# Second attention: four key steps added up before their sum, by GpSimd and DVE

## The chip, the cores and the metric

The kernel runs on one core of a Trainium2 chip. The metric is the device time of one execution in microseconds (us). TensorE (PE in the profile, its weight loads PEld), VectorE (DVE), ScalarE (ACT), GpSimd (POOL) and SyncE (SP, which only issues transfers here) run side by side and meet at semaphores.

## What is computed

Two layers work on x of shape (2, 2048, 256). The first is a linear attention gated by a transformer block with causal softmax attention and a mixture of experts. The second, which the change touches, is this (float32, 16 heads, real and imaginary halves of 16 kept as one head width of 32):

```python
xn = _layernorm(x, axis=-1)
scores = (einsum('bhnd,bhmd->bhnm', q_r, k_r) + einsum('bhnd,bhmd->bhnm', q_i, k_i)) / sqrt(hd)
scores = where(causal, scores, -inf)
probs = softmax(scores, axis=-1)
out = concatenate([einsum('bhnm,bhmd->bhnd', probs, v_r), einsum('bhnm,bhmd->bhnd', probs, v_i)], -1)
s = out @ Wo
g = silu(x_n @ quantized_kernel + bias + (x_n @ a) @ b)
x = x + s * g
```

## The kernel before

The stages run one after another: preparation and the linear attention, the first softmax attention (`narrow_attention`, to about 1290 us), gate, experts and projection, then `wide_attention` (about 2300 to 3410 us), and `finish`, which divides by the softmax sums, projects and adds.

`wide_attention` treats 2 batches of 16 heads as 8 groups of four heads (HG = 4). A unit (g, u) is a group and a block of 512 queries (QB); there are 32 units. A step (unit, kc) is one tile of 128 keys of a unit; unit u has 4u + 4 of them, 320 in all, the last four on the diagonal, where only 512, 384, 256 and 128 query columns are left. The work of a unit, by the names of the schedule:

- S: a score tile with queries on the partitions (line 839, with its mask at 842), 1280 of them; DVE takes the maximum over its keys from PSUM (line 802) and frees one of three PSUM slots. M closes a unit's maxima, T turns them into a row (876, copied at 824), and SyncE's transfers put the row beneath the queries, so that the next products come out with the maximum subtracted.
- ST: a score tile with keys on the partitions for one head (851, 855), four per step; ACT takes its exponential (787) into a slot of `probs`.
- PV: values times probabilities of the step, four heads in four strips of 32 columns of the array (902), into `acc_ps`.
- A: GpSimd adds the probabilities of two neighbouring steps into `added` (751). SM: TensorE sums `added` over keys with a matrix of ones (915); on the diagonal the first 128 columns, which the second step doesn't have, are taken from `probs` (919).
- EV: ACT copies a finished `acc_ps` (764) or `sum_ps` (769) out, and SyncE stores it.

The order of all this is written out ahead by `wide_schedule` (line 477 on), a planner that keeps an end time for each engine and at every turn takes the kind of work on TensorE that could start soonest; each engine then runs its own share of that one list in the list's order. `probs` is a ring of four steps (RING = 4) and `added` has two slots:

```python
mm = pe.matmul(sum_ps[32 * h:32 * h + 32, both:QB], C["ones32"][:, :],
               added[:, totals % 2, h, both:QB], start=kc == 0, stop=False)
```

An exponential into a slot waits for the PV of the step that lay there, and for its addition or, for the first step of a diagonal pair, its sum (`released_by_sums`).

Of the kernel before, what the change touches and what calls it, by code (L numbers as in the profile page):

```python
# [4 lines left out]
F32 = mybir.dt.float32  # L5
# [466 lines left out]
def released_by_sums(step):  # L472
    (g, u), kc = step
    return kc >= 4 * u and kc % 2 == 0


def wide_schedule():
# [31 lines left out]
    exp_end, pv_end, row_at, add_end, sum_end = [], [], {}, [], []  # L509
    at = n_item = n_pair = n_quad = n_sum = of_unit = 0  # L510
# [9 lines left out]

    def lead():
# [6 lines left out]
    while at < len(ahead) or n_quad < len(steps) or 2 * n_sum < len(steps):  # L528
        choice = []
        turn = lambda to: SWITCH if mode != to else 0  # L530
        if at < len(ahead):
# [5 lines left out]
            if g < 2 or n_quad > last_of[g - 2]:  # L537
# [3 lines left out]
                choice.append((start + (500 if lead() > 2 else 0), 0, "S", start))  # L541
        if n_pair < len(steps) * HG:
            s, quad = steps[n_pair // HG], n_pair // HG
            old = quad - RING
            held = old >= 0 and (n_sum if released_by_sums(steps[old]) else len(add_end)) <= old // 2
            if n_pair % (2 * HG) == 2 * HG - 1 and n_sum < quad // 2 - 1:
                held = True
            if s[0] in row_at and quad - n_quad < RING and not held:
                start = max(pe, st_free[n_pair % ST_SLOTS] + 60, row_at[s[0]]) + turn(16)
                choice.append((start, 1, "ST", start))  # L550
        if n_quad < len(steps) and HG * (n_quad + 1) <= n_pair:
# [6 lines left out]
            choice.append((start + 150, 2, "PV", start))  # L558
        if n_sum < len(add_end):
            s = steps[2 * n_sum]  # L560
            ready = add_end[n_sum] + 60
# [4 lines left out]
            choice.append((start + 150, 3, "SM", start))  # L566
        _, _, kind, start = min(choice)
# [20 lines left out]
        elif kind == "ST":  # L588
# [6 lines left out]
            old = quad - RING  # L595
            needs = 0.0 if old < 0 else 220 + max(
                pv_end[old], (sum_end if released_by_sums(steps[old]) else add_end)[old // 2])
# [5 lines left out]
            if h == HG - 1 and quad % 2:  # L603
                body.append(("A",) + s)
                free_tile = sum_end[quad // 2 - 2] if quad // 2 >= 2 else 0.0
                pool = max(pool, act + 100, free_tile + 100) + HG * w * 2.2 + 100
                add_end.append(pool)
        elif kind == "PV":
# [5 lines left out]
            n_quad += 1  # L614
            if s[1] == 4 * s[0][1] + 3:
                body.append(("EV", s[0], 0))
                evictions.append((pe, 0))
        else:
            s = steps[2 * n_sum]
            body.append(("SM",) + s)  # L620
            mode = 32
            pe = start + width2(s) * COLUMN * 4 + 50
            sum_end.append(pe)
            n_sum += 1
            if s[1] == 4 * s[0][1] + 2:
# [5 lines left out]
def wide_attention(nc, tag, C, q_hi, q_lo, k_hi, k_lo, v, out, sums):  # L631
# [13 lines left out]
    steps = [(unit, kc) for unit in units for kc in range(4 * unit[1] + 4)]  # L645
# [3 lines left out]
    with Ctx(nc, tag) as c:  # L649
# [3 lines left out]
        probs = c.sb("probs", [P, RING, HG, QB], F32)  # L653
        added = c.sb("added", [P, 2, HG, QB], F32)
# [25 lines left out]
        add_done = c.sem("add_done")  # L680
        sum_done = c.sem("sum_done")
# [57 lines left out]
        def _(pool):  # L739
            pairs = n = 0  # L740
            for ev in body:
                if ev[0] == "ST":
                    pairs += 1
                elif ev[0] == "A":
                    _, (g, u), kc = ev
                    off = max(0, kc - 4 * u) * P
                    quad = pairs // HG - 1
                    pool.wait_ge(exp_done, pairs)
                    if n >= 2:
                        pool.wait_ge(sum_done, n - 1)  # L750
                    pool.tensor_tensor(added[:, n % 2, :, off:QB], probs[:, (quad - 1) % RING, :, off:QB],  # L751
                                       probs[:, quad % RING, :, off:QB], ALU.add).then_inc(add_done, 1)
# [3 lines left out]
        def _(act):  # L756
# [15 lines left out]
            for ev in body:  # L772
# [7 lines left out]
                if quad >= RING and h == 0:  # L780
                    act.wait_ge(pv_done, quad - RING + 1)
# [1993 lines left out]
```

## Time and profile before

| | us |
|---|---|
| median of 3 runs (3524.80 to 3525.01) | 3524.83 |
| the profiled execution | 3518.76 |
| its span, first instruction to last | 3517.2 |
| matmuls busy in the span | 3023.9 |
| DVE busy | 2043.2 |
| ACT busy | 1594.7 |
| GpSimd busy | 898.5 |

The span is what the hardware profiler recorded of one execution; that execution's own time is 1.6 us more. It was one of those that ran slightly faster than the median of the three timed runs. Busy times of the engines overlap each other, and a matmul's modelled end runs over the start of the next one.

### The profile page before, as it was taken

Reading aid. Unit: us, or ns where it says so; the run is one execution under the profiler, and the core shown is the slowest. Engines: PE = TensorE matmul, PEld = TensorE weight load, DVE = VectorE, ACT = ScalarE, POOL = GpSimd, SP = SyncE. Lnnn points to the kernel's source line nnn. Section 1 sums busy time; section 2 is a strip of 40 time slices with the busy share of each in tenths; the row PEclk is TensorE's granted clock in tenths of the full one; section 3 lists DMA queues with packets and bytes.
Section 4 is the critical chain, followed back from the end, with each engine's and each line's share of the span. In section 5 each row is a group of like instructions: output and inputs, shape, how many; then the busy total and the mean of one; then the engine's idle time right before and its main releaser. Section 6 shows DMA issues by size and latency. Waiting matters only on the chain. (4 is left out here: it accounts for less than half of the span.)

```text
span 3517.2 us, 52224 instructions
## 1 busy us (share of the span) xinstructions
PE 3023.9 (86%) x19331; PEld 1410.5 (40%) x19331; DVE 2043.2 (58%) x4117; ACT 1594.7 (45%) x2665; POOL 898.5 (26%) x448
## 2 busy tenths in 40 slices
PE   4777689999999967669999688869999999999977
PEld 2444323333333326546666434422333333333325
DVE  4778588888888814500000155467657757757625
ACT  1433246666666642213222244425465565565550
POOL 1322100000000001610000212014565465465544
PEclk8998689999999987889999889979999999999988
DMA  7111401201222033412121235440220220210018
GB/s 236 49 57 50 97 9 35 43 15 36 43 40 43 11 69 49 151 57 87 57 86 57 81 121 167 144 99 7 58 55 8 61 45 18 61 37 26 7 48 216
DMA packets 176812, 231.99 MB, mean 66 GB/s; under 512 B 28858, under 2 KB 134141, under 8 KB 173920
## 3 DMA queue, kind: packets, MB, share of 16 engines
q1 hardware_dynamic: 160320, 198.05, 21.2%
q0 software_dynamic: 8704, 22.27, 1.9%
q10 hardware_dynamic: 7584, 8.92, 1.3%
q8 instruction: 131, 2.15, 0.3%
q14 instruction: 73, 0.60, 0.1%
HBM read 138.51 MB, written 93.06 MB: 66 GB/s over the span
## 5 line engine op out<-in xcount | busy, mean ns | idle before, releaser
L802 DVE TENSOR_REDUCE at_part<-at_s 128x1 f32<-128x512 f32 (+3 forms) x1280 | 693.7, 604 | 361.2 <-PE at_s L842 178.1
L787 ACT ACTIVATE at_probs<-at_st 128x512 f32<-128x512 f32 (+3 forms) x1280 | 599.0, 545 | 497.7 <-PE at_st L851 264.3
L351 DVE TENSOR_REDUCE at_part<-at_s 128x1 f32<-128x512 f32 (+3 forms) x1280 | 687.7, 603 | 125.1 <-PE at_s L389 75.8
L751 POOL TENSOR_TENSOR at_added<-at_probs 128x2048 f32<-128x2048 f32 (+2 forms) x160 | 586.2, 3666 | 606.3 <-ACT at_probs L787 606.1
L333 ACT ACTIVATE at_probs<-at_st 128x1024 f32<-128x1024 f32 (+3 forms) x640 | 542.8, 895 | 341.6 <-PE at_st L408 201.2
L389 PE MATMUL at_s<-at_kT,at_qT 48*128 48x512 f16 (+3 forms) x1280 | 371.8, 370 | 51.4 <-DMA at_kT<-klo 21.6
L839 PE MATMUL at_s<-at_kT,at_qT 96*128 96x512 f16 (+3 forms) x1280 | 384.5, 354 | 35.5 <-DMA at_kT<-klo 21.8
L851 PE MATMUL at_st<-at_qT,at_kT 98*128 98x512 f16 (+3 forms) x1280 | 387.9, 353 | 30.9 <-DMA at_qT<-at_strip 16.3
L465 PE MATMUL at_acc<-at_probs,at_v 128*32 128x512 f32 (+3 forms) x2560 | 312.1, 562 | 12.9 <-ACT at_otile L320 12.7
L902 PE MATMUL at_acc<-at_probs,at_v 128*32 128x512 f32 (+3 forms) x2560 | 299.5, 542 | 0.2 <-ACT at_otile L764 0.2
L408 PE MATMUL at_st<-at_qT,at_kT 50*128 50x512 f16 (+3 forms) x1280 | 275.0, 364 | 13.4 <-ACT at_probs L333 7.0
L2272 DVE TENSOR_TENSOR ex_ot<-ex_bank,lin_qf_all 128x512 f32<-128x512 f32 x32 | 22.1, 692 | 450.2 <-PE ex_bank L2302 450.2
L1855 POOL TENSOR_TENSOR aa_a<-aa_a,aa_r 128x1024 f32<-128x1024 f32 x8 | 18.8, 2345 | 934.2 <-DMA aa_r<-inverse 934.2
L389 PEld LDWEIGHTS at_s<-at_kT,at_qT 48*128 48x128 f16 x1280 | 101.6, 94 | 386.5 <-DVE at_part L351 335.1
L851 PEld LDWEIGHTS at_st<-at_qT,at_kT 98*128 98x128 f16 x1280 | 116.9, 97 | 317.4 <-ACT at_probs L787 227.8
L2302 PE MATMUL ex_bank<-lin_w,ex_hT 128*128 128x256 f32 x1024 | 224.5, 380 | 7.0 <-ACT ex_hT L2254 7.0
L2293 PE MATMUL ex_bank<-ex_xT,lin_w 128*128 128x512 f32 x512 | 223.1, 594 | 1.6 <-ACT ex_xT L2246 1.6
L839 PEld LDWEIGHTS at_s<-at_kT,at_qT 96*128 96x128 f16 x1280 | 118.6, 97 | 238.5 <-DVE at_part L802 159.8
L2302 PEld LDWEIGHTS ex_bank<-lin_w,ex_hT 128*128 128x128 f32 x1024 | 193.9, 190 | 43.0 <-ACT ex_hT L2254 13.6
L2254 ACT ACTIVATE ex_hT<-ex_bank,ex_b 128x512 f32<-128x512 f32 x128 | 87.5, 687 | 232.4 <-PE ex_bank L2293 232.4
L2573 PE MATMUL p_bank<-p_xT,p_w 128*128 128x512 f32 x256 | 128.6, 666 | 28.9 <-ACT p_xT L2435 28.9
L2293 PEld LDWEIGHTS ex_bank<-ex_xT,lin_w 128*128 128x128 f32 x512 | 96.8, 190 | 118.5 <-issue 101.6
(289 smaller groups left out, 3544.6 us busy)
## 6 DMA issues: line engine op xcount, KB each, us to landing
at_v<-v SPq DMA_DIRECT2D x16, 1024.0 KB, 17.7
att<-at_otile SPq DMA_DIRECT2D x64, 256.0 KB, 2.4
lin_w<-in_W SPq DMA_DIRECT2D x16, 1024.0 KB, 11.0
exp_in<-all_zeros SPq DMA_DIRECT2D x1, 8192.0 KB, 28.8
v<-pr_vt SPq DMA_DIRECT2D x32, 256.0 KB, 3.1
ex_xin<-exp_in SPq DMA_DIRECT2D x8, 1024.0 KB, 6.2
exp_out<-ex_ot POOLq DMA_DIRECT2D x32, 256.0 KB, 2.6
v<-p_vt SPq DMA_DIRECT2D x32, 256.0 KB, 4.7
```

Of the source, the lines that this page charges most:

```text
L333: act.activation(probs[:, quad % RING, heads_down * p:heads_down * (p + 1), off:QB], st_ps[n % st_slots][:, :, off:QB], ACT.Exp, scale=EXP ...
L351: dve.tensor_reduce(part[:, w % 2, qt * HG + h, j:j + 1], s_ps[n % S_SLOTS][:, 0:width], AX.X, ALU.max).then_inc(item_free, 1)
L389: mm = pe.matmul(place[:, 0:width], QT[g % 2][rows, h // heads_down, q0:q0 + P], KT[g % 2][rows, h // heads_down, j * QB:j * QB + width], ...
L465: mm = pe.matmul(acc_ps[32 * h:32 * h + 32, off:QB], V[g % 2][:, kc, 32 * h:32 * h + 32], probs[:, quads % RING, h, off:QB], start=kc == 0 ...
L751: pool.tensor_tensor(added[:, n % 2, :, off:QB], probs[:, (quad - 1) % RING, :, off:QB], probs[:, quad % RING, :, off:QB], ALU.add).then_i ...
L787: act.activation(probs[:, quad % RING, h, off:QB], st_ps[n % ST_SLOTS][:, off:QB], ACT.Exp, scale=EXP_SCALE).then_inc(exp_done, 1)
L802: dve.tensor_reduce(part[:, w % 2, qt * HG + h, j:j + 1], s_ps[n % S_SLOTS][:, 0:width], AX.X, ALU.max).then_inc(item_free, 1)
L839: mm = pe.matmul(place[:, 0:width], QT[g % 2][0:K, h, q0:q0 + P], KT[g % 2][0:K, h, j * QB:j * QB + width], start=True, stop=not diagonal)
L851: mm = pe.matmul(place[:, off:QB], KT[g % 2][0:K + 2, h, kc * P:(kc + 1) * P], QT[g % 2][0:K + 2, h, u * QB + off:(u + 1) * QB], start=Tru ...
L902: mm = pe.matmul(acc_ps[32 * h:32 * h + 32, off:QB], V[g % 2][:, kc, 32 * h:32 * h + 32], probs[:, quads % RING, h, off:QB], start=kc == 0 ...
L2293: mm = pe.matmul(d[:, :], w1[k][:, n, f * P:(f + 1) * P], xT[:, n, cb * QB:(cb + 1) * QB], start=n == 0, stop=n == NF - 1)
L2302: mm = pe.matmul(d[:, t * D:(t + 1) * D], hT[cb][:, n, (2 * m + t) * P:(2 * m + t + 1) * P], w2[k][:, n, :], start=n == 0, stop=n == NFF - 1)
```

## The change

The sums are taken once for four steps. GpSimd still makes an addition for each pair of steps (160), but in place: into the slot of the pair's first step, once the value product of that step has read it. DVE then adds the total of the second pair to that of the first, also in place (C, 80 joins, from column 256 on where the group lies on the diagonal). SM takes the slot of the group's first step, always 512 columns wide, 80 times; the separate products of 128 columns go. `probs` has six slots in place of four and two of `added`: two, used in turn, for the first steps of groups, and four for the three other steps, in rotation. The planner gets C as an event that it places by the engines' end times, when the second addition has ended or when nothing else can go on; A is placed when the exponentials of both steps and the first one's PV are placed. A score tile of a later unit is put off when the lead is over 3 (before: 2), and PV loses a handicap of 150 ns against ST.

```diff
+def slot_of(quad):
+    group, role = divmod(quad, 4)
+    return group % 2 if role == 0 else 2 + (3 * group + role - 1) % 4
+
+def slot_user_before(quad):
+    group, role = divmod(quad, 4)
+    if role == 0:
+        return quad - 8 if group >= 2 else None
+    n = 3 * group + role - 1 - 4
+    return n // 3 * 4 + n % 3 + 1 if n >= 0 else None
...
+    def join(any_time):
+        nonlocal dve
+        n = len(join_end)
+        if 2 * n + 1 < len(add_end) and (any_time or add_end[2 * n + 1] + 200 <= max(dve, pe)):
+            w = width2(steps[4 * n + 2])
+            dve = max(dve, add_end[2 * n + 1] + 100) + HG * w * 1.05 + 70
+            join_end.append(dve)
+            body.append(("C",) + steps[4 * n + 2])
+            return True
+        return False
...
-                choice.append((start + (500 if lead() > 2 else 0), 0, "S", start))
+                choice.append((start + (500 if lead() > 3 else 0), 0, "S", start))
...
-            choice.append((start + 150, 2, "PV", start))
+            choice.append((start, 2, "PV", start))
...
-        probs = c.sb("probs", [P, RING, HG, QB], F32)
-        added = c.sb("added", [P, 2, HG, QB], F32)
+        probs = c.sb("probs", [P, 6, HG, QB], F32)
...
+                    second = n // 2 * 4 + n % 2 * 2 + 1
+                    total = probs[:, slot_of(second - 1), :, off:QB]
+                    pool.wait_ge(exp_done, HG * (second + 1))
+                    pool.wait_ge(pv_done, second)
+                    pool.tensor_tensor(total, total, probs[:, slot_of(second), :, off:QB],
+                                       ALU.add).then_inc(add_done, 1)
...
+                old = slot_user_before(quad)
+                if h == 0 and old is not None:
+                    group, role = divmod(old, 4)
+                    if role == 0:
+                        act.wait_ge(sum_done, group + 1)
+                    elif role == 2:
+                        act.wait_ge(join_done, group + 1)
                     else:
-                        act.wait_ge(add_done, (quad - RING) // 2 + 1)
+                        act.wait_ge(add_done, 2 * group + role // 2 + 1)
+                        act.wait_ge(pv_done, old + 1)
...
+                if ev[0] == "C":
+                    _, (g, u), kc = ev
+                    off = max(0, kc - 4 * u) * P
+                    total = probs[:, slot_of(4 * joins), :, off:QB]
+                    dve.wait_ge(add_done, 2 * joins + 2)
+                    dve.tensor_tensor(total, total, probs[:, slot_of(4 * joins + 2), :, off:QB],
+                                      ALU.add).then_inc(join_done, 1)
...
-                    pe.wait_ge(add_done, totals + 1)
+                    pe.wait_ge(join_done, totals + 1)
                     for h in range(HG):
-                        mm = pe.matmul(sum_ps[32 * h:32 * h + 32, both:QB], C["ones32"][:, :],
-                                       added[:, totals % 2, h, both:QB], start=kc == 0, stop=False)
...
+                        mm = pe.matmul(sum_ps[32 * h:32 * h + 32, :], C["ones32"][:, :],
+                                       probs[:, slot_of(4 * totals), h, :], start=kc == 0, stop=kc == 4 * u)
```

How the order of instructions moves shows best on two engines. First DVE, in the fifth of the eight groups of heads, across the maxima of two units (at_part: the maxima; at_strip: the row; lines of before):

```order
L802 TENSOR_REDUCE at_part<-at_s 128x1 [waits at1_item_ready] x4
L824 COPY at_strip<-at_s 8x512 [waits at1_row_ready1,at1_item_ready]
L802 TENSOR_REDUCE at_part<-at_s 128x1 [waits at1_strip_ready,at1_item_ready]
L802 TENSOR_REDUCE at_part<-at_s 128x1 [waits at1_item_ready] x59
L809 TENSOR_REDUCE at_rowmax<-at_part 128x16 [waits at1_item_free]
L812 TENSOR_SCALAR at_shift<-at_rowmax 128x16 [waits at1_max_done]
L815 SCALAR_TENSOR_TENSOR at_shift<-at_rowmax,at_shift 128x16 [waits at1_hi_done]
L802 TENSOR_REDUCE at_part<-at_s 128x1 [waits at1_item_ready] x4
```

Before, DVE does nothing there but maxima. The same place after the change (at_probs<-at_probs is a join; its lines lie 44 further down):

```order
L846 TENSOR_REDUCE at_part<-at_s 128x1 [waits at1_item_ready] x3
L840 TENSOR_TENSOR at_probs<-at_probs 128x2048 [waits at1_add_done]
L846 TENSOR_REDUCE at_part<-at_s 128x1 [waits at1_item_ready]
L868 COPY at_strip<-at_s 8x512 [waits at1_row_ready1,at1_item_ready]
L846 TENSOR_REDUCE at_part<-at_s 128x1 [waits at1_strip_ready,at1_item_ready]
L846 TENSOR_REDUCE at_part<-at_s 128x1 [waits at1_item_ready] x5
L840 TENSOR_TENSOR at_probs<-at_probs 128x4x256 [waits at1_add_done]
L846 TENSOR_REDUCE at_part<-at_s 128x1 [waits at1_item_ready] x23
L840 TENSOR_TENSOR at_probs<-at_probs 128x2048 [waits at1_add_done]
L846 TENSOR_REDUCE at_part<-at_s 128x1 [waits at1_item_ready] x17
L840 TENSOR_TENSOR at_probs<-at_probs 128x2048 [waits at1_add_done]
L846 TENSOR_REDUCE at_part<-at_s 128x1 [waits at1_item_ready] x13
```

Joins stand among the maxima, each behind the semaphore of GpSimd's additions, with 7 to 23 maxima between one and the next.

Second TensorE, the last unit's value products and sums at the end of the attention (32x384 and so on: one head's strip, its query columns), before:

```order
L902 MATMUL at_acc<-at_probs,at_v 32x384 [waits at1_exp_done]
L902 MATMUL at_acc<-at_probs,at_v 32x384 x3
L902 MATMUL at_acc<-at_probs,at_v 32x256 [waits at1_exp_done]
L902 MATMUL at_acc<-at_probs,at_v 32x256 x3
L902 MATMUL at_acc<-at_probs,at_v 32x128 [waits at1_exp_done]
L902 MATMUL at_acc<-at_probs,at_v 32x128 x3
L915 MATMUL at_sum<-at_added,all_ones 32x384 [waits at1_add_done,at1_sum_ready]
L915 MATMUL at_sum<-at_added,all_ones 32x384 x3
L919 MATMUL at_sum<-at_probs,all_ones 32x128 x4
L915 MATMUL at_sum<-at_added,all_ones 32x128 [waits at1_add_done]
L915 MATMUL at_sum<-at_added,all_ones 32x128 x3
L919 MATMUL at_sum<-at_probs,all_ones 32x128 x4
```

and after:

```order
L895 MATMUL at_st<-at_qT,at_kT 128x128 [waits at1_exp_done]
L899 MATMUL at_st<-all_mask_kq,all_ident 128x128
L946 MATMUL at_acc<-at_probs,at_v 32x256 [waits at1_exp_done]
L946 MATMUL at_acc<-at_probs,at_v 32x256 x3
L946 MATMUL at_acc<-at_probs,at_v 32x128 [waits at1_exp_done]
L946 MATMUL at_acc<-at_probs,at_v 32x128 x3
L957 MATMUL at_sum<-at_probs,all_ones 32x512 [waits at1_join_done,at1_sum_ready]
L957 MATMUL at_sum<-at_probs,all_ones 32x512 x3
```

Two sums with four sets of products have become one of full width, which waits for the join.

## Rows read from the trace of the kernel before

**Rows 1.** The page: span, busy time and share of each engine.
```profile
span 3517.2 us, 52224 instructions
...
PE 3023.9 (86%) x19331; PEld 1410.5 (40%) x19331; DVE 2043.2 (58%) x4117; ACT 1594.7 (45%) x2665; POOL 898.5 (26%) x448
```

**Rows 2.** Table of stretches: the second attention.
```profile
core 0: us, PE busy (x) PEld busy (x) DVE busy (x) ACT busy (x) POOL busy (x), PEclk, DMA share, GB/s
2330.00:3410.00 1080.00, 1046.08 (x8000) 375.91 (x7997) 716.75 (x1373) 621.54 (x1342) 586.23 (x160) 0.99 0.13 33
```

**Rows 3.** Groups by line and form, 2284 to 3412 us; idle and releaser last.
```profile
L802 DVE TENSOR_REDUCE at_part<-at_s 128x1 f32<-128x512 f32 x896 | 571.7, 684 | 196.9 <-PE at_s L839 174.3 <-PE at_s L842 16.6
L787 ACT ACTIVATE at_probs<-at_st 128x512 f32<-128x512 f32 x896 | 475.3, 611 | 343.3 <-PE at_st L851 264.3 <-PE at_st L855 74.5 <-POOL at_added L751 1.7
L751 POOL TENSOR_TENSOR at_added<-at_probs 128x2048 f32<-128x2048 f32 x96 | 435.3, 4536 | 336.2 <-ACT at_probs L787 336.0
...
L915 PE MATMUL at_sum<-at_added,all_ones 128*32 128x512 f32 x768 | 100.9, 597 | 0.2
...
L915 PE MATMUL at_sum<-at_added,all_ones 128*32 128x384 f32 x256 | 26.9, 492 | 0.3 <-POOL at_added L751 0.3
L919 PE MATMUL at_sum<-at_probs,all_ones 128*32 128x128 f32 x512 | 25.7, 273 | 0.0
...
L915 PE MATMUL at_sum<-at_added,all_ones 128*32 128x128 f32 x256 | 13.5, 283 | 0.1
```

**Rows 4.** Waits in the second attention: total us, times, longest us.
```profile
POOL at_added L751 <- ACT at_probs L787: 606.1, 150, 117.7
...
PEld at_st L851 <- ACT at_probs L787: 227.5, 432, 1.6
...
PEld at_s L839 <- DVE at_part L802: 151.8, 357, 3.4
```

**Rows 5.** Timeline of TensorE's matmuls: start us, us, what.
```profile
2652.32 0.64 PE L902 MATMUL at_acc<-at_probs,at_v 128*32 128x256 f32 x8
...
2652.77 1.04 PE L915 MATMUL at_sum<-at_added,all_ones 128*32 128x512 f32 x8
...
2657.53 0.38 PE L839 MATMUL at_s<-at_kT,at_qT 96*128 96x512 f16 x1
...
2657.74 0.38 PE L851 MATMUL at_st<-at_qT,at_kT 98*128 98x512 f16 x1
...
2661.03 0.38 PE L839 MATMUL at_s<-at_kT,at_qT 96*128 96x512 f16 x1
...
2661.34 1.07 PE L902 MATMUL at_acc<-at_probs,at_v 128*32 128x512 f32 x8
...
2662.34 0.82 PE L839 MATMUL at_s<-at_kT,at_qT 96*128 96x512 f16 x3
```

**Rows 6.** Timeline of GpSimd, 2446 to 2462 us: start, us; idle before in brackets.
```profile
2451.47 9.17 POOL L751 TENSOR_TENSOR at_added<-at_probs 128x2048 f32<-128x2048 f32 x2 [0.26 <-ACT at_probs L787]
2461.14 4.55 POOL L751 TENSOR_TENSOR at_added<-at_probs 128x2048 f32<-128x2048 f32 x1 [0.50 <-ACT at_probs L787]
```

**Rows 7.** DVE groups by form, whole execution: operations with two SBUF inputs.
```profile
L1432 DVE TENSOR_TENSOR pr_fr<-pr_fr,pr_fs 128x512 f32<-128x512 f32 x32 | 22.1, 692 | 1.1
...
L2494 DVE TENSOR_TENSOR all_x_all<-p_fg,p_xs 128x256 f32 x24 | 10.2, 425 | 0.8
...
L1444 DVE SCALAR_TENSOR_TENSOR pr_kr<-pr_kr,pr_ke 128x1024 f32<-128x1024 f32 x8 | 9.7, 1218 | 0.0
```

**Rows 8.** Timeline of DVE and GpSimd in the last stage, from 3440 us: start, us.
```profile
3441.34 4.51 POOL L1855 TENSOR_TENSOR fi_a<-fi_a,fi_r 128x2048 f32<-128x2048 f32 x1 [5.38 <-DMA fi_r<-inverse]
...
3442.82 3.31 DVE L2645 TENSOR_TENSOR fi_o<-fi_o,all_x_all 128x256 f32<-128x256 f32 x1 [0.49 <-DVE fi_o L2642]
```

**Rows 9.** Line 1401 in the first stage: ns min/median/max of its 16 additions.
```profile
L1401 DVE TENSOR_TENSOR pr_qr<-pr_qr,pr_qc x16: 691/692/1747, 71.0 to 367.2; 128x512 f32<-128x512 f32 x16
```

More of the change, by code:

```diff
@@ L519, in evict, with released, add @@
             free[k] = act
+    def released(quad):
+        old = slot_user_before(quad)
+        if old is None:
+            return 0.0
+        group, role = divmod(old, 4)
+        if role == 0:
+            return sum_end[group] if group < len(sum_end) else None
+        if role == 2:
+            return join_end[group] if group < len(join_end) else None
+        add = 2 * group + role // 2
+        return max(add_end[add], pv_end[old]) if add < len(add_end) and old < len(pv_end) else None
+    def add():
+        nonlocal pool
+        n = len(add_end)
+        second = n // 2 * 4 + n % 2 * 2 + 1
+        if HG * (second + 1) <= len(exp_end) and second - 1 < len(pv_end):
+            w = width2(steps[second])
+            pool = max(pool, exp_end[HG * second + HG - 1] + 100, pv_end[second - 1] + 220) + HG * w * 2.2 + 100
+            add_end.append(pool)
+            body.append(("A",) + steps[second])
+    def join(any_time):
[8 more added lines that the diff above has]
+        return False
     def lead():
@@ L526, in lead @@
         return place[first] + of_unit / count[first] - place[unit] - kc / (4 * unit[1] + 4)
-    while at < len(ahead) or n_quad < len(steps) or 2 * n_sum < len(steps):
+    while at < len(ahead) or n_quad < len(steps) or 4 * len(sum_end) < len(steps):
+        join(False)
         choice = []
@@ L540, in wide_schedule @@
                 start = max(pe, ready) + turn(16)
-                choice.append((start + (500 if lead() > 2 else 0), 0, "S", start))
+                choice.append((start + (500 if lead() > 3 else 0), 0, "S", start))
         if n_pair < len(steps) * HG:
             s, quad = steps[n_pair // HG], n_pair // HG
[L544 to L548, printed above, removed]
+            if s[0] in row_at and released(quad) is not None:
                 start = max(pe, st_free[n_pair % ST_SLOTS] + 60, row_at[s[0]]) + turn(16)
@@ L566, in wide_schedule @@
             choice.append((start + 150, 3, "SM", start))
+        if not choice or min(choice)[3] > dve + 1000:
+            if join(True):
+                continue
         _, _, kind, start = min(choice)
@@ L602, in wide_schedule @@
             n_pair += 1
[L603 to L607, printed above, removed]
+            add()
         elif kind == "PV":
@@ L796, in _ @@
         def _(dve):
-            n, w = 0, 0
+            n, w, joins = 0, 0, 0
             for ev in body:
-                if ev[0] == "S":
+                if ev[0] == "C":
[5 more added lines that the diff above has]
+                                      ALU.add).then_inc(join_done, 1)
+                    joins += 1
+                elif ev[0] == "S":
                     _, (g, u), qt, h, j, width = ev
@@ L908, in _ @@
                     _, (g, u), kc = ev
-                    first = max(0, kc - 4 * u) * P
-                    both = max(0, kc + 1 - 4 * u) * P
                     if kc == 0 and place_of[ev[1]]:
                         pe.wait_ge(sum_ready, place_of[ev[1]])
-                    pe.wait_ge(add_done, totals + 1)
+                    pe.wait_ge(join_done, totals + 1)
                     for h in range(HG):
-                        mm = pe.matmul(sum_ps[32 * h:32 * h + 32, both:QB], C["ones32"][:, :],
-                                       added[:, totals % 2, h, both:QB], start=kc == 0, stop=False)
-                    if both > first:
-                        for h in range(HG):
-                            mm = pe.matmul(sum_ps[32 * h:32 * h + 32, first:both], C["ones32"][:, :],
-                                           probs[:, 2 * totals % RING, h, first:both],
-                                           start=False, stop=kc == 4 * u + 2)
+                        mm = pe.matmul(sum_ps[32 * h:32 * h + 32, :], C["ones32"][:, :],
+                                       probs[:, slot_of(4 * totals), h, :], start=kc == 0, stop=kc == 4 * u)
                     mm.then_inc(sum_done, 1)
```

51 lines of the change are left out of this document (19 added, 32 removed).

## Prediction

> **What bounds the kernel now.** I began with the page's totals: matmuls fill 86% of the span, DVE 58%, ACT 45%, GpSimd 26% [rows 1]. Such shares mix stages, so the next view was the table of stretches. The second attention runs from 2330 to about 3410 us, and in those 1080 us TensorE is busy 1046 us at a granted clock of 0.99, DVE 717, ACT 622, GpSimd 586 [rows 2]. TensorE is the busiest, but "busy" flatters it, because the modelled end of one matmul runs over the start of the next. So I read starts: four value products of full width (one step) start at 2661.34 and the next product starts at 2662.34, 1.00 us later, where the row shows 1.07 [rows 5]. The 256-column step at 2652.32 is followed by its neighbour of the same kind after 0.45 us [rows 5], so 512 columns in four heads stream in about 0.85 us. The waits say who holds TensorE up: weight loads of key-side scores wait for ACT's exponentials 227.5 us in total and those of row scores wait for DVE's maxima 151.8 us [rows 4]. Most of that is a load ready early, but it tells that both loops turn with little slack: TensorE bounds the stage, and DVE and ACT are close behind it. GpSimd only waits for exponentials, 606 us [rows 4].
>
> **What the change removes.** Before, 160 additions feed 160 sums. 96 of them are full width (x768 in the rows, 8 records each), 32 have 384 columns and 32 have 128, and with the last two kinds go 64 products of 128 columns taken from the slots [rows 3]. In full widths that is (96×512 + 32×384 + 32×128 + 64×128) / 512 = 144, at 0.85 us 122.4 us. After, 80 full widths, 68.0 us. Streaming falls by **54.4 us**. Second, TensorE changes between products that use 128 columns of the array and those that use 32. The order holds 372 visits to the second kind before and 278 after. A visit costs about 0.10 us going in (2661.03 to 2661.34 is 0.31, a full-width score product alone about 0.21, by the starts 2657.53 and 2657.74) and 0.15 coming out (1.00 less 0.85) [rows 5]. 94 visits at 0.25 us: **23.5 us**. Together 78 us leave TensorE.
>
> **What it adds on DVE.** There are 80 joins, 48 over 2048 elements per partition and 32 over 1024. DVE's additions of two SBUF tiles take 425 ns for 256 and 692 for 512 [rows 7], a slope of 1.04 ns, so 2.29 us and 1.23 us (a two-input operation of 1024 took 1218 ns [rows 7]). That is 48×2.29 + 32×1.23 = 149 us on an engine with 363 us to spare in the stretch: DVE rises from 66% to about 80% of it. In the order a join stands between two row maxima. Behind it are the maxima that free three PSUM slots, each 0.68 us of DVE work [rows 3], so TensorE can run about 2.0 us of them ahead before it stops; the order also puts value products and key-side scores there. A join that starts at once thus costs TensorE between nothing (other products stand there) and, where the slots are already used up, its whole length: 0 to 149 us for all. The waits for maxima are short ones, 0.4 us on the mean of 357 [rows 4], so the slots mostly are not used up; what is left of a wide join beyond them is 0.3 us, 14 us for 48, and I take **10 us**.
>
> **The joins against GpSimd.** This is the term that decides. DVE's addition at 3442.82 reads two SBUF tiles and lasted 3.31 us, and GpSimd's multiplication, begun at 3441.34, ended at 3445.85, 0.3 us before it: DVE stood until GpSimd was through [rows 8]. Elsewhere the same kind of DVE operation has a median of 692 ns and a longest of 1747, beside GpSimd's 1.27 us operations [rows 9]. The row maxima read PSUM and keep 684 ns while GpSimd adds all around them [rows 3]. So a join that reaches DVE after GpSimd has begun its next addition can stand for up to 4.54 us [rows 3], with everything queued behind it: maxima, the shift row, and through them TensorE's scores. The Trainium skill (SBUF — State Buffer, "Who interferes with whom") says that a DVE instruction with two SBUF inputs and a GpSimd instruction that reads SBUF exclude each other for the whole instruction, whichever began first. By that rule the loser is sometimes GpSimd; a late addition there is covered by its idle time of 606 us.
>
> How many joins are caught? In the order every join stands ahead of the last exponentials that the next addition needs, so the join is meant to come first. What GpSimd's rows show is how soon an addition follows another: at 2451.47 two ran on without a gap, after a gap of 0.26 us [rows 6]. Of the 79 gaps in which a join would now lie (behind every second addition), I counted 12 under 0.3 us, 13 under 0.7 us (one maximum), and 38 under 2.3 us (one join). No row shows joins among them; the bounds are 0 and 38 caught. The new order makes room for the join, and 66 of the 160 additions stand in it directly behind a value product that they now wait for, which starts them later; so I take 13, nearer the low end. Each holds DVE 4.5 us longer, of which the three slots cover 2.0: 2.5 us of TensorE, within bounds of 0 (the slots and other products cover it) and 4.5 (slots already used up by the join). 13 × 2.5 = **33 us** lost.
>
> **Small terms.** The in-place addition costs nothing in itself: GpSimd's in-place multiplication of 2048 took 4.51 us at 3441.34 [rows 8], the addition into another tile 4536 ns [rows 3]. Its wait for the first step's value product is hidden by GpSimd's idle time; if that cover goes, the exponential into the slot is late next. Six slots stand in place of four and two, and a slot is needed again four of the moving ones later, while ACT waited for GpSimd 1.7 us in all before (the row of its exponentials [rows 3]): nothing, with a risk of some us if a join is late, for the slot of a group's third step waits for the join. SyncE's queue gets the same stores. At the end of the last unit the chain gains a join of 1.23 us and about 0.4 us of wider sum: 2 us, exposed, because all after it is unchanged and starts when the attention has ended.
>
> **Sum.** −78 + 10 + 33 + 2 = −33 us. The profiled execution took 3518.8 us, so 3486 on its own terms; the runs' median is 6.1 us above it, 3524.8, and that gives **3492 us**. A measurement of this kernel can tell about 0.2%, 7 us, from no change.
>
> **The rivals.**
> - *Nothing is caught* (the joins slip in as the order intends, at most two or three meet an addition): −78 + 12 = −66, 3459 us. For it: each join is ahead of the next addition's inputs in the order, and 41 of 79 gaps were longer than a join. Against: DVE takes up a join only after the maxima queued before it, which runs later than TensorE's place in the order.
> - *The shared access takes it back*: GpSimd is busy in 54% of the stretch [rows 2]; if the joins fall on it as by chance, or as the 38 short gaps say, 38 stand the full 4.5 us: 38 × 2.5 = 95, and −78 + 95 + 12 = +29, 3554 us, slower. It decides from (78 − 12) / 2.5, about 26 joins, on; with 13 to 26 the gain only shrinks. For it: the row with 3.31 us; against it: the new order's places. The Trainium skill (Perfetto Trace Analysis, "Optimizing Scalar/DVE Operations") warns that since GpSimd and DVE share a read port, moving work between them might not help; taken whole, that is this rival.
> - *TensorE was not the bound*: the loops of scores, exponentials and maxima set the pace (the 227.5 and 151.8 us [rows 4]), and the 78 us turn into waits; DVE's extra 149 us eats what is left. Then 3525, no change. Against it: TensorE sat idle only 34 us of 1080 [rows 2], and the sums wait for hardly anything.
>
> **How the numbers follow.** Forecast (5 to 25 joins caught, so 3471 to 3521): 0.60. Nothing caught, 3459 to 3471: 0.14. Not the bound, within 7 us of 3525: 0.12. Shared access, 3528 to 3575: 0.14. The range of 8 in 10 leaves out the lowest part of the second and most of the last: 3462 to 3534. Faster by over 0.2% holds the second case and nearly all of the first (0.73), the same 0.12 and a sliver of the first (0.12 in all), slower the rest, 0.15.
>
> **What would show it.** Right: about 80 full-width sums of 1.05 us busy each where there were 167 us of sums; DVE some 150 us up for joins plus 40 to 80 us of stretched ones; joins whose median is near 2.3 us but whose longest is near 6.8; row maxima still 684 ns. Wrong: joins all at 2.3 us and a stage shorter by over 60 us, or joins with a mean above 4 us and long waits of row scores for DVE; or TensorE's idle time in the stage up by 60 us with unstretched joins. My forecast falls with the count of caught joins above all.

## The result and the profile after

| | us |
|---|---|
| changed kernel, median of 4 runs (3558.05 to 3563.67) | 3560.32 |
| kernel before, median of 4 runs | 3524.92 |
| ratio to the kernel before | 1.0098 (95%: 1.0080 to 1.0115) |
| its profiled execution, and its span | 3563.67, 3561.7 |

The forecast was a gain of 33 us (3492); the kernel lost 35. The measured time lies near the second rival's number (3554), but as the traces show not by its mechanism. From here on "the stage" is the second attention from its first row maximum to the last copy of a sum: 2303.7 to 3408.7 us before, 1105.0 us long, and 2317.5 to 3453.9 after, 1136.4 us, so 31.4 us longer. What follows it kept its length (108.5 and 107.8 us).

The page of the changed kernel, its totals (before: [rows 1]):

```profile
PE 3018.1 (85%) x18179; PEld 1403.5 (39%) x18179; DVE 2219.9 (62%) x4197; ACT 1589.8 (45%) x2665; POOL 927.2 (26%) x448
```

The stage in the table of stretches, before and after (columns as in [rows 2]). TensorE's busy time fell, DVE's rose from 731 us of 1105 to 907 of 1136, and the mean granted clock (1.00 is TensorE's full speed) fell from 0.99 to 0.94. Before:

```profile
core 0: us, PE busy (x) PEld busy (x) DVE busy (x) ACT busy (x) POOL busy (x), PEclk, DMA share, GB/s
2303.70:3408.70 1105.00, 1059.46 (x8062) 381.23 (x8060) 731.27 (x1408) 622.49 (x1344) 586.23 (x160) 0.99 0.15 36
```

and after:

```profile
2317.50:3453.90 1136.40, 1034.60 (x6910) 363.11 (x6908) 907.25 (x1488) 616.98 (x1344) 613.09 (x160) 0.94 0.14 35
```

Groups by line and form in the changed kernel, 2284 to 3460 us (columns as in [rows 3]; 846 maxima, 783 GpSimd's additions, 840 joins, 957 sums, 856 and 859 the two operations of 16 elements per partition that make a unit's shift row):

```profile
L846 DVE TENSOR_REDUCE at_part<-at_s 128x1 f32<-128x512 f32 x896 | 575.1, 684 | 82.5 <-PE at_s L883 62.1 <-PE at_s L886 16.2
...
L783 POOL TENSOR_TENSOR at_probs<-at_probs 128x2048 f32<-128x2048 f32 x96 | 451.0, 4702 | 318.9 <-ACT at_probs L823 166.2 <-PE at_acc L946 152.7
...
L840 DVE TENSOR_TENSOR at_probs<-at_probs 128x2048 f32<-128x2048 f32 x48 | 112.9, 2352 | 59.8 <-POOL at_probs L783 59.6
...
L957 PE MATMUL at_sum<-at_probs,all_ones 128*32 128x512 f32 x640 | 88.7, 626 | 9.7 <-DVE at_probs L840 7.9 <-ACT at_stile L801 1.8
...
L840 DVE TENSOR_TENSOR at_probs<-at_probs 128x1024 f32<-128x1024 f32 x32 | 39.0, 1218 | 25.9 <-POOL at_probs L783 25.9
...
L856 DVE TENSOR_SCALAR at_shift<-at_rowmax 128x16 f16<-128x16 f32 x32 | 30.8, 963 | 1.1
...
L859 DVE SCALAR_TENSOR_TENSOR at_shift<-at_rowmax,at_shift 128x16 f16<-128x16 f32 x32 | 26.1, 816 | 1.1
```

The sums are near the forecast (80 of 1.05 us, 84 us): 88.7 us busy where there were 167. So are the joins: 152 us, 2352 ns the wide ones (2.29 us forecast), 1218 ns the narrow (1.23), and the maxima keep 684 ns. What stands out are the last two rows. They took 464 and 180 ns each before (14.9 and 5.7 us in all) and take 963 and 816 now, 45 us above the 0.18 us that they take undisturbed. The same two operations in the kernel before, by groups:

```profile
L812 DVE TENSOR_SCALAR at_shift<-at_rowmax 128x16 f16<-128x16 f32 x32 | 14.9, 464 | 1.1
...
L815 DVE SCALAR_TENSOR_TENSOR at_shift<-at_rowmax,at_shift 128x16 f16<-128x16 f32 x32 | 5.7, 180 | 1.1
```

The waits of the changed kernel, 2330 to 3446 us (columns as in [rows 4]):

```profile
POOL at_probs L783 <- PE at_acc L946: 350.9, 53, 120.7
PEld at_s L883 <- DVE at_part L846: 277.1, 547, 6.1
...
DVE at_probs L840 <- POOL at_probs L783: 79.2, 21, 12.4
...
ACT at_probs L823 <- DVE at_probs L840: 19.1, 7, 4.3
```

GpSimd now waits for value products, 351 us, as its in-place additions must; TensorE's row scores wait 277 us for DVE's maxima (151.8 before); DVE stands 79 us in front of joins; ACT's exponentials stand 19 us for joins, because a join frees the slot of a group's third step (before, ACT waited 1.7 us for GpSimd in all). One place shows what a dry spell looks like. Timeline of the changed kernel around 2766 us (start us, us, what; idle before in brackets):

```profile
2765.11 0.39 PE L883 MATMUL at_s<-at_kT,at_qT 96*128 96x512 f16 x1
...
2766.50 0.18 DVE L856 TENSOR_SCALAR at_shift<-at_rowmax 128x16 f16<-128x16 f32 x1
2766.67 8.99 POOL L783 TENSOR_TENSOR at_probs<-at_probs 128x2048 f32<-128x2048 f32 x2 [8.81 <-PE at_acc L946]
2766.72 4.52 DVE L859 SCALAR_TENSOR_TENSOR at_shift<-at_rowmax,at_shift 128x16 f16<-128x16 f32 x1
...
2769.00 0.11 PEld L883 LDWEIGHTS at_s<-at_kT,at_qT 96*128 96x128 f16 x2 [0.84 <-issue]
2769.00 0.60 PE L883 MATMUL at_s<-at_kT,at_qT 96*128 96x512 f16 x2
2771.15 0.68 DVE L846 TENSOR_REDUCE at_part<-at_s 128x1 f32<-128x512 f32 x1
...
2771.89 0.29 PE L883 MATMUL at_s<-at_kT,at_qT 96*128 96x128 f16 x1 [2.28 <-DVE at_part L846]
...
2774.08 0.61 PE L895 MATMUL at_st<-at_qT,at_kT 98*128 98x512 f16 x1
```

GpSimd's addition starts at 2766.67, released by a value product (the row holds two additions, 8.99 us together). The second operation of the shift row reads two SBUF tiles, starts at 2766.72 and stays until the first addition is over, 4.52 us. The score product at 2769.00 fills the last slots, then TensorE stands 2.28 us for a maximum. And the same score product of 512 columns that showed 0.39 us ahead of the spell shows 0.61 behind it: the granted clock has gone from its upper level (2.4 GHz) to its lower (1.2 GHz). Counted from such timelines, TensorE had 5 gaps of over 0.8 us in the stage before, 7 us in all, and has 20 now, 52 us; 13 of them, 33 us, end with a row maximum or a shift row. (One more gap, of 10 to 11 us, waits for the first unit's shift row and stands at the head of the stage in every kernel here; all counts leave it out.) By the trace's clock records TensorE was granted its lower level for 30 us of the stage before, and for 133 us now.

Four more of the 20 gaps, 12 us, stand in front of value products, and there were none of this kind before. They lead to a join by another way:

```profile
2627.40 1.22 DVE L840 TENSOR_TENSOR at_probs<-at_probs 128x1024 f32<-128x1024 f32 x1
...
2628.65 0.60 ACT L823 ACTIVATE at_probs<-at_st 128x512 f32<-128x512 f32 x1 [4.28 <-DVE at_probs L840]
2629.14 0.59 ACT L796 ACTIVATE at_otile<-at_acc 128x512 f32<-128x512 f32 x1
...
2629.78 1.94 PE L946 MATMUL at_acc<-at_probs,at_v 128*32 128x512 f32 x8 [3.78 <-ACT at_otile L796]
```

The exponential waits 4.28 us for the slot that the join frees, ACT's copy of the finished accumulator stands behind it in ACT's queue, and TensorE waits 3.78 us for the copy.

### The profile page after: what moved, and what is told of

Same layout as the page of the kernel before. It is cut to its first block and busy times, and to the rows that moved or that the text cites. A ratio compares the mean times of both kernels' runs of the same rounds, so it can differ in the third digit from the quotient of the medians.

```text
span 3561.7 us, 50000 instructions
## 1 busy us (share of the span) xinstructions
PE 3018.1 (85%) x18179; PEld 1403.5 (39%) x18179; DVE 2219.9 (62%) x4197; ACT 1589.8 (45%) x2665; POOL 927.2 (26%) x448
## 5 line engine op out<-in xcount | busy, mean ns | idle before, releaser
L783 POOL TENSOR_TENSOR at_probs<-at_probs 128x2048 f32<-128x2048 f32 (+2 forms) x160 | 613.1, 3838 | 609.1 <-PE at_acc L946 351.6
L883 PE MATMUL at_s<-at_kT,at_qT 96*128 96x512 f16 (+3 forms) x1280 | 409.4, 367 | 63.8 <-DVE at_part L846 38.3
L895 PE MATMUL at_st<-at_qT,at_kT 98*128 98x512 f16 (+3 forms) x1280 | 407.1, 364 | 34.2 <-ACT at_probs L823 16.1
L895 PEld LDWEIGHTS at_st<-at_qT,at_kT 98*128 98x128 f16 x1280 | 124.4, 100 | 205.8 <-ACT at_probs L823 118.1
L840 DVE TENSOR_TENSOR at_probs<-at_probs 128x2048 f32<-128x2048 f32 (+1 forms) x80 | 151.9, 1899 | 85.6 <-POOL at_probs L783 85.5
```

The costliest lines, as they stand in the source:

```text
L783: pool.tensor_tensor(total, total, probs[:, slot_of(second), :, off:QB], ALU.add).then_inc(add_done, 1)
L883: mm = pe.matmul(place[:, 0:width], QT[g % 2][0:K, h, q0:q0 + P], KT[g % 2][0:K, h, j * QB:j * QB + width], start=True, stop=not diagonal)
L895: mm = pe.matmul(place[:, off:QB], KT[g % 2][0:K + 2, h, kc * P:(kc + 1) * P], QT[g % 2][0:K + 2, h, u * QB + off:(u + 1) * QB], start=Tru ...
```

## The experiments

Their two theories: **theory 1**, the shift row's operations are caught by GpSimd's additions, TensorE runs dry and loses its clock; **theory 2**, DVE had no room for the joins, either for their length or for the waits in front of them. The chips of the three groups differ (the kernel before took 3583, 3586 and 3529 us beside them, since earlier stages took longer on the first two: the stage began at 2363 to 2381 us there, at 2304 to 2321 elsewhere); so the ratio is always against the kernel before on the same chip, and the stage's length, which came out as 1136.4 and 1136.2 us for the changed kernel on two chips, compares across them. Times in the expectations of the first four runs count from 3525 for the kernel before; by their ratios the four came to 3518, 3521, 3533 and 3608 on those terms.

**Without joins, and with their waits alone** (e1_no_join, e2_join_wait_only). On DVE:

```diff
-                    dve.wait_ge(add_done, 2 * joins + 2)
-                    dve.tensor_tensor(total, total, probs[:, slot_of(4 * joins + 2), :, off:QB],
-                                      ALU.add).then_inc(join_done, 1)
```

with sums and slots waiting for `add_done` in its place; in the second run the wait stays and `dve.nop().then_inc(join_done, 1)` stands for the join. Both kernels leave the second pair's total out of the sums.

> The joins are left out (the second pair's total of each group of four steps is not counted); order of the work, additions and 80 sums stay, the sums and the slots wait for GpSimd's additions. Theory 1 (the two small operations that make the shift row, each with its SBUF access shut while GpSimd adds, run TensorE dry and the granted clock falls with it): those operations are as long as in the changed kernel (about 46 us more than 0.18 us each), the clock stays near 0.94 in the stage, time 3535 to 3560. Theory 2 (DVE had no room for 150 us of joins, or stood 85 us at them for late additions): the stage is shorter by 60 us or more against the changed kernel, time 3470 to 3500.

> As the run without joins, but DVE still waits at the joins' places for the additions (the join itself is a no-operation, so the second pair's total is not counted). It parts the length of the joins from the wait in front of them. If the wait decides, it is within 10 us of the changed kernel (3550 to 3565); if the 150 us of work decide, it is within 10 us of the run without joins. Theory 1 expects both runs near 3550.

```profile
2369.10:3466.70 1097.60, 1013.67 (x6910) 362.38 (x6908) 768.39 (x1408) 614.96 (x1343) 585.30 (x160) 0.95 0.15 36
```

```profile
2366.90:3464.70 1097.80, 1013.11 (x6910) 362.10 (x6907) 768.43 (x1408) 614.87 (x1343) 585.33 (x160) 0.96 0.15 36
```

(The stage in the table of stretches, columns as above; the changed kernel's row is the one that starts with 2317.50.) The stage took 1097.6 and 1097.8 us, 39 under the changed kernel, ratios 0.998 (0.997 to 0.999) and 0.999 (0.997 to 1.000). In the second run DVE still stood 47 us for GpSimd's additions at the joins' places, as its waits show (the other 4.7 us are in front of line 867):

```profile
DVE at_part L845 <- POOL at_probs L783: 42.5, 7, 11.5
```

That cost nothing. The 152 us of joins, with all that meets them (GpSimd's additions held up, exponentials that wait for a slot), cost 39; these runs don't part them further, but the gaps for ACT's copies fell from 12 to 2 us. Neither theory's number was met: the time lies between the two. The shift rows stayed 47 us too long as theory 1 has it, TensorE's gaps fell only from 52 to 38 us, and yet 39 us went. Even with no joins on DVE at all, the sums once per four steps give no more than 7 us over the kernel before, in that order of work.

**Guarding the shift row** (e3_guard): GpSimd's queue gets one more wait.

```diff
-            n = 0
+            n = rows = 0
             for ev in body:
-                if ev[0] == "A":
+                if ev[0] == "M":
+                    rows += 1
+                    pool.wait_ge(shift_ready, rows)
+                elif ev[0] == "A":
```

> The changed kernel with one more wait: GpSimd takes no addition that stands behind a unit's maxima in the order before the shift row of that unit is made. Theory 1: most of the 18 long operations of the shift row (1 to 4.5 us) go back to 0.18 us, save those that meet an addition begun earlier, the gaps of TensorE in front of row scores mostly go, the clock rises towards 0.98, time 3520 to 3540. Theory 2: no gain, 3555 to 3570, since DVE's load and its waits at joins stay, and additions come later.

The two operations in the guarded kernel:

```profile
L859 DVE TENSOR_SCALAR at_shift<-at_rowmax 128x16 f16<-128x16 f32 x32 | 15.6, 486 | 1.1
...
L862 DVE SCALAR_TENSOR_TENSOR at_shift<-at_rowmax,at_shift 128x16 f16<-128x16 f32 x32 | 5.7, 179 | 1.1
```

```profile
2376.00:3484.50 1108.50, 1022.06 (x6910) 358.19 (x6908) 876.92 (x1488) 614.99 (x1343) 613.49 (x160) 0.96 0.14 36
```

The 45 us became 10 (the second operation is never caught, the first only by an addition that had begun), the stage 1108.5 us, 28 shorter, ratio 1.002 (1.001 to 1.004) where the changed kernel stood at 1.010. Theory 1 had said this, theory 2 no gain. The caught shift rows are a cause. (Three joins were caught here, up to 6.59 us, where the changed kernel has one.)

**Both** (e6_no_join_guard), on the next chip, and beside it the changed kernel once more (e5_changed_again).

> The changed kernel itself, beside this group's runs of the kernel before, so that the others of the group can be held against it. Second attention from its first row maximum to the last copy of a sum: within 5 us of 1136 (1105 before), ratio near 1.010.

> No joins, and GpSimd waits for the shift row (both edits together; the second pair's total is not counted). If the joins' length on DVE (39 us of the stage in the run without joins) and the caught shift rows (28 us in the guarded run) are two costs that add, the stage falls from 1136 to about 1070, ratio near 0.99. If they are one cost (the same dry spells of TensorE), it stays at 1090 or more.

```profile
2363.00:3499.20 1136.20, 1032.77 (x6910) 363.70 (x6908) 907.26 (x1488) 617.00 (x1343) 613.69 (x160) 0.95 0.14 35
```

```profile
2381.40:3441.60 1060.20, 995.83 (x6910) 355.92 (x6908) 729.70 (x1408) 612.95 (x1343) 585.31 (x160) 0.98 0.15 38
```

The changed kernel: 1136.2 us, ratio 1.0105 (1.007 to 1.014). With both edits the stage took 1060.2 us, 76 less, where 39 and 28 alone make 67: two costs that add, with a little more. Its ratio is 0.990 (0.986 to 0.993), with the second pair's total left out of the sums. The clock went with them: 51 us at the lower level, 17 us of gaps.

**GpSimd makes the joins** (e4_pool_joins): the same lines in GpSimd's queue.

> GpSimd makes the 80 joins as well, in the same places of the order; DVE has none. GpSimd gets 48 x 4.5 + 32 x 2.3 = 290 us more and is busy 900 of about 1130 us. Theory 1: more of GpSimd's work means that more of the shift row's operations are caught and sums and slots wait longer: 3560 to 3600. Theory 2: DVE is free, 3500 to 3530.

```profile
2364.60:3555.80 1191.20, 1040.31 (x6910) 366.00 (x6908) 789.85 (x1408) 616.87 (x1344) 874.85 (x240) 0.93 0.14 33
```

1191.2 us, ratio 1.024 (1.021 to 1.026): worse than on DVE by 55 us. 46 us of TensorE's gaps now stand in front of sums, for GpSimd, and the shift rows are caught for 68 us. Theory 2's number (DVE free, so faster) fell, and theory 1's range (to 3600) was just passed.

**The planner's weights alone** (e7_before_weights), in the kernel before:

```diff
-                choice.append((start + (500 if lead() > 2 else 0), 0, "S", start))
+                choice.append((start + (500 if lead() > 3 else 0), 0, "S", start))
-            choice.append((start + 150, 2, "PV", start))
+            choice.append((start, 2, "PV", start))
```

> The kernel before with only the planner's two weights of the change (lead over 3, value products without their 150 ns handicap); sums, additions and slots as before. If the new weights alone bunch TensorE's work and make dry spells, the stage is 10 to 30 us over 1105; if the loss comes from joins and caught shift rows alone, it is within 8 us of 1105.

1122.1 us against 1105.0, ratio 1.006 (1.004 to 1.008): 17 us lost with nothing else changed, and hardly by gaps (10 us, 3 more) or clock (37 us at the lower level, 7 more); where the other 10 us went isn't shown. Part of that may not carry over to the new order, whose plan is another. The changed kernel with the old weights was not run, since its queues would wait on each other in a circle, so what the weights cost there stays open.

**A planner that knows of it** (e8_planned_guard): the guarded kernel, with these lines in the schedule, S put off from a lead of 4, joins taken 1 us after their additions.

```diff
+            pool_from = max(pool, shifted + 100, exp_end[HG * second + HG - 1] + 100, pv_end[second - 1] + 220)
...
+            dve = max(dve, add_end[2 * n + 1] + 100)
+            if pool_from <= dve < pool:
+                dve = pool
+            dve += HG * w * 1.05 + 140
...
-                dve += 700
-                made = dve
+                if pool_from <= dve < pool:
+                    dve = pool
+                dve += 700
+                made = shifted = dve
```

> The guarded kernel with a planner that knows of it: an addition starts behind the shift row, a join or a shift row that would meet a running addition is put behind its end, a join is taken 1 us after its additions, row scores are put off from a lead of 4. Caught shift rows should be under 5 us in all. If order is what is left of the loss, the stage falls under the 1108 of the guarded run, to 1080 to 1100, ratio 0.99 to 1.00; if DVE's load of joins is, it stays near 1108.

1093.9 us, ratio 0.998 (0.997 to 1.000): level with the kernel before. The caught shift rows were 18 us and not under 5. 28 us of the gaps stand in front of sums, for joins, 7 of which were now caught.

**Splitting the joins** (e9_split_join on that kernel, e12_guard_split on the guarded one): each in two halves of two heads, the second behind the next maximum.

```diff
+                if rest and (ev[0] in ("C", "SM", "M", "T") or ev[0] == "ST" and ev[3] == 0 or rest[1]):
+                    half(*rest[0], slice(2, 4)).then_inc(join_done, 1)
+                    rest = None
```

> The kernel with guard and planner that knows of it (stage 1094), each join cut into two of two heads, the second taken behind the next row maximum where one comes before a sum, a new step or the end of a unit. If it is the unbroken hold of 2.3 us that starves TensorE of score slots, the stage falls to 1075 to 1088; if it is DVE's load (150 us and some 100 ns more for each cut), it stays at 1094 or rises by up to 10.

> The guarded kernel in the changed kernel's own order (stage 1108.5), with split joins. Hold theory: 1085 to 1100; load theory: 1108 to 1118.

Both answers that were expected (the unbroken hold of a join, or DVE's load) missed: 1174.7 us (ratio 1.021, 1.018 to 1.023) and 1224.7 us in its single run, 81 and 116 us **longer**. First the half joins by form in e9_split_join, then one of them on its timeline:

```profile
L846 DVE TENSOR_TENSOR at_probs<-at_probs 128x1024 f32<-128x1024 f32 x96 | 182.8, 1916 | 49.9 <-POOL at_probs L792 49.7
```

```profile
2734.62 4.51 POOL L792 TENSOR_TENSOR at_probs<-at_probs 128x2048 f32<-128x2048 f32 x1 [2.96 <-PE at_acc L964]
2734.96 5.25 DVE L846 TENSOR_TENSOR at_probs<-at_probs 128x1024 f32<-128x1024 f32 x1
...
2740.74 0.50 PE L901 MATMUL at_s<-at_kT,at_qT 96*128 96x384 f16 x1 [3.82 <-DVE at_part L864]
```

1916 ns on the mean for 1024 elements, where 1218 is undisturbed; 21 pieces took over 3.4 us, 15 of them second halves (24 and 21 in the other split kernel), against 7 joins before the split and one in the changed kernel (5.51 us at 2914). This is the caught join of my forecast, made to happen: the half that comes a maximum later meets GpSimd's next addition (begun at 2734.62, the half at 2734.96 stands 5.25 us) and TensorE waits 3.82 us for a slot. Of the split kernel's 79 us of gaps 51 stand in front of sums, which now wait for the second half, and 22 in front of row scores. The split cost 81 us, clock included (168 us at the lower level, 84 before); how much of that is caught pieces and how much the later end of each join isn't parted. The Trainium skill (Perfetto Trace Analysis, "Optimizing Scalar/DVE Operations") says that where DVE isn't saturated but makes bubbles elsewhere, breaking up instructions may let work be completed sooner; these runs disagree (DVE was busy 895 of 1094 us before the split), for pieces that can be shut out one by one.

**Two more orders** (e10_sum_slack, e11_join_600), each one number in the planner of e8: a sum held ready 0.8 us after its join; joins taken 0.6 us after their additions.

> The same kernel, unsplit, with a planner that holds a sum ready 0.8 us after its join and not 0.06. TensorE's 28 us of gaps in front of sums should fall under 15; if they are what is left, the stage is 1075 to 1088 and the ratio to the kernel before near 0.993; if other gaps take their place, 1090 or more.

> The same kernel with joins taken 0.6 us after their additions in the plan (1.0 before). A plain variation of the order: if the stage hangs on the order more than on what it must do, it moves by 10 us or more either way; if not, it stays within 8 us of 1094.

```profile
2320.80:3397.70 1076.90, 1005.10 (x6910) 366.44 (x6908) 889.34 (x1488) 616.91 (x1344) 611.65 (x160) 0.96 0.15 37
```

1104.7 us (ratio 1.001, 1.000 to 1.002) and 1076.9 us, ratio **0.993** (0.991 to 0.995). In the first the gaps in front of sums fell from 28 to 4 us as expected, and the stage still grew by 11 us: other costs took their place. The second, 3504.7 us beside 3528.9, beats the kernel before, with 7 joins caught and 27 us of gaps in front of sums. A number of 0.4 us in a plan moves the stage by 17 us: what is left depends on the order; which meeting costs what isn't shown.

| kernel | stage us | gaps over 0.8 us | at the lower clock, us | stage less gaps less half the last |
|---|---|---|---|---|
| before | 1105.0 | 7 | 30 | 1083 |
| changed | 1136.4 | 52 | 133 | 1018 |
| no joins | 1097.6 | 38 | 99 | 1010 |
| guard | 1108.5 | 36 | 95 | 1025 |
| no joins, guard | 1060.2 | 17 | 51 | 1017 |
| joins on GpSimd | 1191.2 | 102 | 160 | 1009 |
| before, new weights | 1122.1 | 10 | 37 | 1093 |
| planned guard | 1093.9 | 30 | 84 | 1022 |
| split joins on it | 1174.7 | 79 | 168 | 1012 |
| split joins, guard | 1224.7 | 114 | 177 | 1023 |
| sum slack | 1104.7 | 22 | 91 | 1037 |
| joins at 0.6 us | 1076.9 | 33 | 87 | 1000 |

The last column is a rough estimate: it takes half of the time at the lower level (1.2 GHz against 2.4) as lost, though some of the gaps lie in that time and TensorE isn't always busy there. It is the ledger of the case: all kernels that sum once per four steps have 1000 to 1037 us of work and short waits, the two that sum once per two have 1083 and 1093. By this estimate the change did take some 65 us out of TensorE; gaps (+45) and the lower clock (103 us more of it, so about +51) took 96 back.

## Why the prediction was wrong

The step that failed is what DVE costs TensorE, 43 us of the sum: 33 for caught joins, 10 for the joins' length, and nothing for any other DVE operation or for the clock. The runs showed one caught join, 39 us for the joins' length and what hangs on it, and 28 us for a victim that the sum didn't have. The items in turn:

- **What the change removes**, −78 us: the ledger's −65, though rough, is near it (and near −68, with the joins' length). No run shows the 78 by themselves: with joins left out and the guard in, the stage was 45 us shorter than before, with 10 us more of gaps and 21 us more at the lower clock. One slip in the working: 0.45 us for 256 columns makes 0.90 for 512, not 0.85. But from one full step to the start of the next of its kind the trace of before has 0.86 us at least and 0.88 in the median of 52, so the sum hardly moves.
- **The joins against GpSimd**, +33 us. I took 13 joins caught. One was. In 30 of the 160 additions it was the other way round: the join had begun first and GpSimd's addition stood behind it. I had named that side and covered it with GpSimd's idle time, but didn't let it lower the count. So this term was far too high; put right alone, it would have moved the forecast further from the result. The split joins show that caught ones do occur and what one can cost (3.82 us of TensorE in the example above, where I had taken 2.5).
- **Who else reads SBUF beside GpSimd**: missing from the sum. By the same rule the shift row's two small operations stand still, and 18 of them did, for 45 us of DVE and 28 us of the stage. The trace of before had it: line 812 had a mean of 464 ns and a longest of 3072 beside its usual 180 (below: ns min/median/max), while I looked only at operations that the change adds. In the example above an addition that a value product released met the shift row; additions wait for value products only since the change.

```profile
L812 DVE TENSOR_SCALAR at_shift<-at_rowmax x32: 178/180/3072, 2310.9 to 3377.8; 128x16 f16<-128x16 f32 x32
```

- **The joins' length**, +10 us: 39 by the run without joins (its clock and gaps included, and what GpSimd and ACT lose by joins). The forecast priced only the maxima behind a join; the sums in front of which TensorE waits for a join it did not price, and the exponentials that wait for a slot it had as a risk of some us. Which of these holds most of the 39 isn't shown.
- **The clock**: nowhere in the sum. I read 0.99 in [rows 2] as given. In the table above the time at the lower level grows with the gaps, and from before to after 45 us of gaps came with about 51 us lost to the clock. That is an estimate; no run holds the clock still.
- **The new weights** of the planner: costed at nothing and not named as a part of their own. In the kernel before they cost 17 us.
- **The rivals.** "The shared access takes it back" gave the number, 3554 for 3560, by luck: it needs 38 caught joins, and the shared access accounts for 28 us by another victim. "TensorE was not the bound" is partly right: without joins and with all of DVE's waits, the stage gained 7 us only. The range, to 3534, was too narrow for a change whose costs hang on how a thousand instructions meet: I had given 0.14 to the times in which the result fell.

## What to carry to other kernels

Before moving work to DVE beside a busy GpSimd, list every DVE instruction that can be shut out, the tiny ones on a serial path first, and look at the longest of each in the trace, not at the mean. If TensorE is near its bound, price a gap twice, once for itself and once for the clock behind it (by this case's ledger, about as much again). And where a planner sets the order, put the exclusion into the plan and try a few of its numbers on the chip: here guard, plan and one such number together turned +1.0% into −0.7%.

## What the runs showed of the hardware

- An operation of 16 elements per partition, 0.18 us alone, took up to 4.52 us while GpSimd added two SBUF tiles (line 859, two SBUF inputs). The first of the pair, with one SBUF input and an f16 output (line 856), was caught as well, up to 4.27 us, as in this row pair of the changed kernel (columns: ns min/median/max):

```profile
L856 DVE TENSOR_SCALAR at_shift<-at_rowmax x32: 178/180/4270, 2324.7 to 3393.8; 128x16 f16<-128x16 f32 x32
```

```profile
L859 DVE SCALAR_TENSOR_TENSOR at_shift<-at_rowmax,at_shift x32: 178/180/4517, 2324.9 to 3394.0; 128x16 f16<-128x16 f32 x32
```

  The Trainium skill (SBUF — State Buffer, "Who interferes with whom") names both kinds, two SBUF inputs and the two-port modes that `tensor_scalar` can enter, and exempts `tensor_reduce`; the trace agrees: the small reductions of line 853, which read SBUF, kept 181 to 220 ns, and the maxima, which read PSUM, 684 ns. Which mode the first operation ran in the trace doesn't tell.
- GpSimd is shut out in its turn: its additions, 4.52 us in the median, took up to 6.55 us, about one join more, where the join had begun first:

```profile
3081.41 2.28 DVE L840 TENSOR_TENSOR at_probs<-at_probs 128x2048 f32<-128x2048 f32 x1
...
3081.53 6.55 POOL L783 TENSOR_TENSOR at_probs<-at_probs 128x2048 f32<-128x2048 f32 x1 [1.04 <-PE at_acc L946]
```

  By their mean (4702 against 4536 ns) that is 16 us for the 96 wide ones. No run parts its cost from that of the joins' length.
- Behind a gap of 2.28 us on TensorE the clock was at its lower level (0.61 us for 0.39). Not every such gap did that: behind one of 2.13 us, at 3241, the same score product took 0.39 us again. I had not expected single gaps of this size to matter in a stage that is otherwise 90% busy.
- Cutting a DVE operation to let another in between made things worse by 81 and 116 us. Pieces were caught 21 and 24 times, 15 and 21 of them second halves, which came when GpSimd had begun again; and sums waited for the later end.
